# Later weights loaded from ScalarE's queue, weight products placed inside step 0, and a third buffer of turned rows

## The chip, the cores and the metric

The kernel runs on one core of one Trainium2 chip. That core has a TensorE for matrix products (PE in the rows), a VectorE (DVE), a ScalarE (ACT), a GpSimd (POOL) and a SyncE (SP) that only issues transfers, with 16 DMA engines behind them. The metric is the device time of one execution in microseconds. One profiled execution gives the trace that all rows are from; the times of three other runs are given beside it.

## The reference

The reference is one layer in three parts over `x`, 64 sequences of 64 tokens with 256 channels:

```python
x = x + _L0_xattn_ref(_layernorm(x, axis=-1), ctx_1024, mask, Wq, bq, Wk, bk, Wv, bv, Wo, bo)   # 16 heads, rotary, causal, 256 context rows
x = x + _L0_attn_ref(_layernorm(x, axis=-1), Wq, Wk, Wg1, Wg2, Wv, Wg, bg, Wo)                  # gated linear attention
x = x + _L0_ffn_ref(_layernorm(x, axis=-1), shared_gate, shared_up, shared_down,
                    routed_gate, routed_up, routed_down, Wr, routing_bias)                      # 1 shared + 7 routed experts, top 2
```

Two facts of it matter below. The keys' gate of the second part is `inputs @ Wg1 @ Wg2`, so a program can multiply the two weights once instead of twice per token. And the value bias `bv` of the first part passes through the softmax unchanged, so `bv @ Wo + bo` is one constant row that is added to the result. Each expert is `silu(x @ gate) * (x @ up) @ down` with 704 hidden channels, and each token's two routed results are added with its two weights.

## The kernel before

**Attention stage.** The 64 sequences go in 32 pairs, 128 tokens each. The work on one pair is cut into pieces (`turn_xn`, `proj_q`, `proj_k01`, `scores0`, ...), and each engine has a function `step(s)` that lists the pieces in a fixed order, each with a lag: `at(s, 2, weigh0)` runs `weigh0` on pair `s - 2`. There are 41 steps. Nothing but these lists and the semaphores sets the order; every engine takes its own list strictly in turn.

A pair starts like this: VectorE takes the statistics of its rows (`x_stats`, L1547), ScalarE makes the reciprocal deviation (L1121, L1123) and the high half of the context rows (`ctx_high`, L1224), GpSimd normalises (`x_norm`, L665) and makes the context's low half (`ctx_low`, L624). SyncE turns the split context rows by a transposing transfer (`turn_ctx`, L415). TensorE turns the normalised rows (`turn_xn`, L735), makes the queries (`proj_q`, L740), and then, with the turned context, the keys and values (`proj_k01`, `proj_k10`, `proj_v0`, `proj_k11`, all at L748). Matrix products are split in a high and a low half of 16 bits.

**Before the first step** each engine has a preamble. SyncE issues the loads in one queue: constants, the first context, `Wk`, `Wv`, their tables (`kv_loaded`), the first rows, the query weights, then 19 loads counted by `start_loaded` (L479: `Wg1`, `Wg2`, `bo` and `Wo` in 16 pieces) and 7 counted by `weights_loaded` (L484). ScalarE loads its table of functions (L1316), waits for `kv_loaded` and makes the high halves of `Wk` and `Wv` (L1319, L1320); VectorE makes the low halves and related copies (L1642 to L1654). TensorE waits for all 19 of `start_loaded`, turns `Wg1` (L1002), multiplies `bv` by `Wo` (L1005, recorded at L740) and `Wg1` by `Wg2` (L1008). VectorE copies and splits these results (L1657 to L1665), and only then comes to `x_stats` of pair 0, since it takes its list in turn.

**Expert stage.** 4096 tokens go through the shared expert in 16 tiles of 256, and 8192 choices (token, expert) through the routed experts in 35 tiles of 256, sorted by expert. The order of the 51 tiles is: tiles 0 to 9 shared, 10 to 44 routed (in each of the last four of these, each half has its own expert), 45 to 50 the last six shared. Each tile has on TensorE `up(t, half 0)`, `down(t - 1)`, `up(t, half 1)`: half 0 is 36 products of 128x256 at L1022, `down` 34 at L1050 to L1055, half 1 is 30 at L1022. In the trace half 1 of a tile and half 0 of the next stand in one row of 66.

The rows of a tile come to TensorE turned: `turn_rows(t)` on SyncE issues two transposing transfers (L531) into `e_rows_t[t % 2]`. It waits until tile `t - 2` has read this buffer (`up_done`, two counts per tile). For routed tiles GpSimd gathers the rows first (L694), and after the tile scatters the results to `choice_out` (L703). When tile 44 is done, GpSimd reads `choice_out` back in 8 transfers of 1 MB each (L721), and VectorE adds these results to the tokens (`combine`, L1907): one group of 8 operations beside tile 46, two beside each of 47, 48 and 49, one beside tile 50. The last transfers store the output (L725 on GpSimd, L562 on SyncE).

Of the kernel before, what the change touches and what calls it, by code (L numbers as in the profile page):

```python
# [6 lines left out]
ALU = mybir.AluOpType  # L7
# [4 lines left out]
F16 = mybir.dt.float16  # L12
# [33 lines left out]
LAST = 6  # L46
WORK = 9140
# [105 lines left out]
def program(nc, stack, x, ctx_in, pad, xWq, xbq, xWk, xWv, xWo, xbo, gWq, gWk, gWg1, gWg2, gWv,  # L153
# [134 lines left out]
    e_rows_t = [place2(2 * DK * R // 2).bitcast(F16).rearrange("p (m n) -> p m n", n=R) for _ in range(2)]  # L288
# [59 lines left out]
    for name in """  # L348
# [10 lines left out]
        route_exp route_mm route_step scores0_done scores1_done shared_hi shared_lo shared_loaded silu_ready  # L359
        slot_mm slots_loaded slots_read split_x2n_done start_loaded start_mm start_ready sum_decay_done  # L360
        sum_step table_ready turn_ctx_done turn_g_done turn_heads0_done turn_heads1_done turn_p00_done
        turn_p01_done turn_p10_done turn_p11_done turn_q_done turn_x1n_done turn_x2n_done turn_xn_done up_done
        v_hi0_done v_hi1_done v_lo0_done v_lo1_done waits_met weigh0_done weigh1_done weigh_g_done
        weights_loaded x1_norm_done x1_rstd_done x1_stats_done x1n_high_done x1n_low_done x2_norm_done
        x2_rstd_done x2_stats_done x2n_copy_done x_norm_done x_rstd_done x_stats_done xn_copy_done y_ready
        y_stored
# [5 lines left out]
    rows_turned = [sem(f"rows_turned{k}") for k in range(2)]  # L372
# [11 lines left out]
    def at(s, lag, op, first=0):  # L384
        if first <= s - lag < NPAIR:
            op(s - lag)
# [9 lines left out]
    def _(sp):  # L396
# [75 lines left out]
        first = [(w_g1, kmaj(gWg1)), (w_g2[0:16, :], gWg2), (b_o, xbo.partition_broadcast(P))]  # L472
        for hp in range(8):
            for a in range(2):
                row = (2 * hp + a) * HC
                first.append((w_o[hp * HC:(hp + 1) * HC, a, :], xWo[row:row + HC, :]))
        assert len(first) == START_DMAS
        for dst, src in first:
            sp.dma_start(dst, src).then_inc(S["start_loaded"], 16)  # L479
        wl = S["weights_loaded"]  # L480
        count = [0]

        def wload(dst, src):
            sp.dma_start(dst, src).then_inc(wl, 16)  # L484
            count[0] += 1

        wload(w_gqk[:, :, 0:P], kmaj(gWq))
        wload(w_gqk[:, :, P:2 * P], kmaj(gWk))
        wload(w_gvg[:, :, 0:D], kmaj(gWv))
        wload(w_gvg[:, :, D:2 * D], kmaj(gWg))  # L490
        wload(w_go, kmaj(gWo))
        wload(w_r, kmaj(Wr))
        wload(b_g[0:SQ, :], gbg.partition_broadcast(SQ))
        assert count[0] == WEIGHT_DMAS
# [50 lines left out]
        turn_tokens(1, 1)  # L545
        for t in range(FIRST):
# [4 lines left out]
            if t + 2 < FIRST:  # L551
                turn_tokens(t + 2, t + 2)
# [16 lines left out]
    def _(pool):  # L569
# [160 lines left out]
    def _(pe):  # L730
# [239 lines left out]

        def step(s):
# [12 lines left out]
            at(s, 0, turn_xn)  # L984
            at(s, 2, weigh1)
# [7 lines left out]
            at(s, 0, proj_k01)  # L993
            at(s, 0, proj_k10)
# [994 lines left out]
```

## Time and profile before

| | us |
|---|---|
| median of 3 runs | 1596.11 |
| lowest and highest of them | 1595.52, 1599.26 |
| profiled execution | 1593.83 |
| its span (first to last instruction) | 1592.0 |
| attention stage, expert stage, in the span | 0 to about 928, about 930 to 1592 |

The profiled execution is 1.83 us longer than its span; this lies around the span and isn't seen in the rows. It is 2.28 us below the median of the runs. Busy time is a sum over the whole span; a row of the timeline gives the start, the time and the idle time of the engine just ahead of it, with what ended that. A transfer's row on SPq (SyncE's queue) is only the time that it takes to issue it; when it lands is in other views.

### The profile page before, as it was taken

How to read it: one execution, taken by the hardware profiler on the slowest of the kernel's cores; microseconds unless marked ns; L12 is line 12 of the kernel's file. 1: busy time of each engine (PE TensorE's matmuls, PEld its weight loads, DVE VectorE, ACT ScalarE, POOL GpSimd, SP SyncE). 2: the span in 40 equal slices, each digit the busy share in tenths (PEclk: the TensorE clock that was granted, in tenths of full speed). 3: DMA queues.
4: the chain of work that ended last, by engine and by line, in shares of the span. 5: the costliest groups of instructions: out<-in, count | busy, mean ns of one | idle time of the engine just before them, and what ended most of it. 6: DMA issues, size and time to landing. Idle time of an engine off the chain costs nothing.

```text
span 1592.0 us, 43384 instructions
## 1 busy us (share of the span) xinstructions
PE 1434.0 (90%) x17186; PEld 1074.6 (68%) x17186; DVE 1085.5 (68%) x1972; ACT 847.2 (53%) x1838; POOL 761.4 (48%) x677
## 2 busy tenths in 40 slices
PE   3788998999999999999999665999999999999987
PEld 1456675666666666666666454887888888887865
DVE  2886889888888888888888459784444444443357
ACT  1566876777778777777687422452323232322221
POOL 1575677777677767676766310002333333332110
PEclk9899999999999999999999678999999999999998
DMA  4586776777677777767685343552422222221182
GB/s 136 115 167 125 148 136 124 141 132 144 137 139 142 137 149 135 150 129 146 119 155 97 74 101 70 139 156 70 74 67 74 68 74 68 74 68 55 38 267 74
DMA packets 464497, 183.62 MB, mean 115 GB/s; under 512 B 414608, under 2 KB 452832, under 8 KB 464304
## 3 DMA queue, kind: packets, MB, share of 16 engines
q1 hardware_dynamic: 454128, 149.25, 47.3%
q0 software_dynamic: 10176, 31.60, 5.7%
q8 instruction: 145, 2.38, 0.6%
q14 instruction: 48, 0.39, 0.1%
HBM read 61.77 MB, written 17.56 MB: 50 GB/s over the span
## 4 chain that ended last, share of the span: by engine, by line
PE 56%; DVE 24%; ACT 11%; issue 4%; DMA 3%; SPq 1%; POOL 1%; DVEq 0%; POOLq 0%
PE ps L1022 22%; PE ps L1050 10%; PE ps L748 9%; DVE experts L1392 6%; ACT experts L1128 4%; PE ps L740 4%; DVE work L1523 4%; ACT experts L1115 3%; PE ps L765 2%; DVE experts L1480 2%; PE ps L735 2%; PE ps L792 2%; DVE experts L1431 1%; DMA work<-token_in 1%; PE ps L1055 1%
## 5 line engine op out<-in xcount | busy, mean ns | idle before, releaser
L1022 PE MATMUL ps<-work,experts 128*128 128x256 f16 (+1 forms) x3630 | 403.7, 272 | 42.1 <-DMA work<-token_in 13.4
L1022 PEld LDWEIGHTS ps<-work,experts 128*128 (+1 forms) x3630 | 340.0, 100 | 97.6 <-issue 15.6
L748 PE MATMUL ps<-experts 128*128 128x512 f16 (+2 forms) x2304 | 363.8, 309 | 31.4 <-DVE work L1536 14.7
L748 PEld LDWEIGHTS ps<-experts 128*128 128x128 f16 x2304 | 198.2, 100 | 174.5 <-DVE work L1536 28.9
L1115 ACT ACTIVATE work<-work 128x768 f16<-128x768 f32 (+1 forms) x134 | 99.3, 741 | 368.5 <-PE ps L1055 234.4
L1128 ACT ACTIVATE experts<-ps,experts 128x256 f32<-128x256 f32 x512 | 203.8, 474 | 74.9 <-DVE experts L1392 74.8
L627 POOL TENSOR_TENSOR experts<-experts 128x1024 f16<-128x1024 f32 x96 | 191.7, 1996 | 61.0 <-ACT experts L1115 61.0
L694 POOL DMA_INDIRECT work<-token_in,work x70 | 68.0, 972 | 309.2 <-DMA work<-work 216.1
L1050 PE MATMUL ps<-experts,work 128*128 (+1 forms) x1530 | 187.8, 276 | 3.7 <-DVE work L1700 3.7
L1050 PEld LDWEIGHTS ps<-experts,work 128*128 128x128 f16 x1530 | 146.9, 99 | 28.7 <-DVE work L1700 4.0
L1392 DVE TENSOR_REDUCE experts<-ps 128x4 f32<-128x1024 f32 x128 | 155.9, 1219 | 12.7 <-PE ps L765 11.7
L1683 DVE SCALAR_TENSOR_TENSOR work<-ps,work 128x768 f32<-128x768 f32 x102 | 84.1, 824 | 115.9 <-PE ps L1022 115.4
L1115 ACT ACTIVATE experts<-experts 128x1024 f16<-128x1024 f32 x128 | 135.9, 1062 | 2.0
L703 POOL DMA_INDIRECT choice_out<-work x70 | 69.4, 992 | 134.9 <-DVE work L1841 123.7
L1696 DVE TENSOR_TENSOR work<-work 128x768 f16<-128x768 f32 x102 | 86.5, 848 | 58.7 <-ACT work L1115 58.7
L1334 ACT ACTIVATE work<-ps 128x768 f32<-128x768 f32 x102 | 82.5, 809 | 80.3 <-PE ps L1022 80.3
L748 PE MATMUL ps<-work,experts 128*128 128x33 f16 x3072 | 88.3, 178 | 23.1 <-issue 16.9
L748 PEld LDWEIGHTS ps<-work,experts 128*128 128x128 f16 x3072 | 86.0, 96 | 28.9 <-issue 28.1
L1841 DVE TENSOR_SCALAR work<-ps 128x512 f32<-128x512 f32 x35 | 24.2, 692 | 108.0 <-PE ps L1055 108.0
L740 PE MATMUL ps<-experts,work 128*128 128x256 f32 (+1 forms) x388 | 93.2, 360 | 2.7 <-ACT work L1115 1.7
L1431 DVE SCALAR_TENSOR_TENSOR experts<-ps,experts 128x512 f32<-128x512 f32 x128 | 88.8, 736 | 8.5 <-PE ps L748 8.5
L624 POOL TENSOR_TENSOR experts<-experts 128x1024 f16<-128x1024 f32 x32 | 72.2, 2256 | 16.6 <-ACT experts L1224 16.6
(211 smaller groups left out, 2184.4 us busy)
## 6 DMA issues: line engine op xcount, KB each, us to landing
experts<-in_ctx SPq DMA_DIRECT2D x32, 512.0 KB, 5.0
experts<-choice_out POOLq DMA_DIRECT2D x8, 1024.0 KB, 13.1
experts<-in_x SPq DMA_DIRECT2D x32, 128.0 KB, 2.3
token_in<-experts SPq DMA_DIRECT2D x32, 128.0 KB, 2.9
work<-in_L_ffn_routed_gate SPq DMA_DIRECT2D x8, 352.0 KB, 3.1
experts<-experts SPq DMA_TRANSPOSE x160, 4.6
work<-in_L_ffn_routed_up SPq DMA_DIRECT2D x8, 320.0 KB, 4.4
out<-x_all POOLq DMA_DIRECT2D x5, 512.0 KB, 3.3
```

The costliest lines, as they stand in the source:

```text
L627: nc.gpsimd.tensor_tensor(probs_s[b][m][:, 1, :], probs[b][:, 4 * m:4 * m + 4, :].rearrange("p s j -> p (s j)"), probs_s[b][m][:, 0, :], A ...
L740: ins = pe.matmul(bank, lhs[k], rhs[k], start=(k == 0), stop=(k == len(lhs) - 1))
L748: ins = pe.matmul(bank, lhs[a][k], rhs[b][k], start=(k == 0 and a + b == 0), stop=(last and k == len(lhs[0]) - 1 and a == 1))
L1022: ins = pe.matmul(out[:, r * n:(r + 1) * n], experts_h[:, e, lo:lo + P], e_rows_t[k][:, b * DK + kk, r * n:(r + 1) * n], start=(kk == 0 an ...
L1050: pe.matmul(out, e_hid_s[a][:, c, rows], experts_h[:, e, at:at + D], start=(c == 0 and a + b == 0), stop=False)
L1115: nc.scalar.activation(dst, src, ACT.Copy).then_inc(done, 1)
L1128: ins = nc.scalar.activation(probs[b][:, s, :], ps[:, r, g * SK:(g + 1) * SK], ACT.Exp, bias=neg_max[b][:, s:s + 1])
L1334: nc.scalar.activation(e_silu, ps_flat[:, 512 + half * HALF:512 + (half + 1) * HALF], ACT.Silu, scale=1 / W_SCALE).then_inc(S["silu_ready" ...
L1392: v.tensor_reduce(neg_max[b][:, 4 * m:4 * m + 4], ps_flat[:, 1024 * m:1024 * m + 1024].rearrange("p (s j) -> p s j", j=SK), AX.X, ALU.max, ...
L1431: v.scalar_tensor_tensor(out=dst.rearrange("p (b j) -> p b j", b=2), in0=bank.rearrange("p (b j) -> p b j", b=2), scalar=b_cols[:, 2 * e + ...
L1683: ins = v.scalar_tensor_tensor(out=e_hid[:, 0:n], in0=ps_flat[:, 2048 + half * HALF:2048 + half * HALF + n], scalar=1 / W_SCALE, in1=e_sil ...
L1696: ins = v.tensor_tensor(low, e_hid[:, 0:n], high, ALU.subtract)
```

## The change

There are three parts.

1. The 19 loads of `start_loaded` and the 7 of `weights_loaded` are issued by ScalarE, right behind its table load and ahead of its first ACTIVATE. SyncE goes from the query weights straight into its steps.
2. TensorE's three weight products leave the preamble. `start_turn` (the two transposes of `Wg1` and the product `bv @ Wo`) stands in step 0 behind `turn_xn`, `start_weight` (`Wg1 @ Wg2`) in step 0 behind `proj_k01`. VectorE's copies and splits become `start_bias` and `start_split` in step 1, behind `masks_of` and behind `q_cos` of pair 0. Some semaphores are merged for this (`shared_hi` into `kv_high`, `shared_lo` into `kv_split`).
3. `e_rows_t` has three buffers instead of two; `turn_rows(t)` waits for tile `t - 3`.

```diff
+NROWS = 3
@@ SyncE
-        first = [(w_g1, kmaj(gWg1)), (w_g2[0:16, :], gWg2), (b_o, xbo.partition_broadcast(P))]
...
-        for dst, src in first:
-            sp.dma_start(dst, src).then_inc(S["start_loaded"], 16)
...
         def turn_rows(t, rows):
-            wait(sp, S["up_done"], t * 2 - 2)
+            wait(sp, S["up_done"], 2 * (t - NROWS) + 2)
             apart(sp)
             for a in range(2):
-                sp.dma_start_transpose(e_rows_t[t % 2][:, :, a * P:(a + 1) * P], rows[a]).then_inc(rows_turned[t % 2], 16)
+                sp.dma_start_transpose(e_rows_t[t % NROWS][:, :, a * P:(a + 1) * P], rows[a]).then_inc(rows_turned[t % NROWS], 16)
-        turn_tokens(1, 1)
+        for t in range(1, NROWS):
+            turn_tokens(t, t)
...
-            if t + 2 < FIRST:
-                turn_tokens(t + 2, t + 2)
+            if t + NROWS < FIRST:
+                turn_tokens(t + NROWS, t + NROWS)
@@ GpSimd
         def residual(p):
-            if p == 0:
-                pool.wait_ge(S["start_ready"], 9)
         def gather(t):
             if t > FIRST:
-                pool.wait_ge(rows_turned[(t - 1) % 2], ((t - 1) // 2 + 1) * 32)
+                pool.wait_ge(rows_turned[(t - 1) % NROWS], ((t - 1) // NROWS + 1) * 32)
@@ TensorE
+        def start_turn(p):
+            pe.wait_ge(S["start_loaded"], 16 * START_DMAS)
+            pe.wait_ge(S["start_ready"], 7)
+            for k in range(DK):
+                pe.transpose(ps[0:16, 0, k * P:(k + 1) * P], w_g1[:, k, :], ident)
+            product(ps[:, 0, D:2 * D], [bv_rows[:, a, :] for a in range(2)], [w_o[:, a, :] for a in range(2)], S["start_mm"])
+
+        def start_weight(p):
+            pe.wait_ge(S["start_ready"], 8)
+            for k in range(DK):
+                ins = pe.matmul(ps[:, 2, k * P:(k + 1) * P], w_g1_t[0:16, k, :], w_g2[0:16, :], start=True, stop=True)
+            ins.then_inc(S["start_mm"], 1)
             at(s, 0, turn_xn)
+            at(s, 0, start_turn, 0, 1)
...
             at(s, 0, proj_k01)
+            at(s, 0, start_weight, 0, 1)
             at(s, 0, proj_k10)
         pe.wait_ge(S["consts_loaded"], 16)
-        pe.wait_ge(S["start_loaded"], 16 * START_DMAS)
...
@@ ScalarE
         act.preload_act_table_set("natural_log_exp_and_others")
+        for dst, src in first:
+            act.dma_start(dst, src).then_inc(S["start_loaded"], 16)
...
         act.wait_ge(S["consts_loaded"], 16)
         act.wait_ge(S["kv_loaded"], 64)
@@ VectorE
+        def start_bias(p):
+            dve.wait_ge(S["start_mm"], 1)
+            dve.wait_ge(S["start_loaded"], 16 * START_DMAS)
+            v.tensor_copy(w_g1_t[0:16], ps[0:16, 0, 0:DK * P].rearrange("p (k n) -> p k n", k=DK))
+            v.tensor_tensor(b_o, ps[:, 0, D:2 * D], b_o, ALU.add).then_inc(S["start_ready"], 1)
+
+        def start_split(p):
+            dve.wait_ge(S["start_mm"], 2)
...
             at(s, 1, masks_of)
+            at(s, 1, start_bias, 0, 1)
...
             at(s, 1, q_cos)
+            at(s, 1, start_split, 0, 1)
```

What the change moves is seen where each engine's instructions stand in a row. TensorE at its beginning, before:

```order
L1002 MATMUL ps<-cst,work 16x128 x2
L740 MATMUL ps<-experts,work 128x256 x2
L1008 MATMUL ps<-work 128x128 x2
L735 MATMUL ps<-cst,experts 128x128 x2
L740 MATMUL ps<-experts 128x256 x2
L748 MATMUL ps<-experts 128x512 x12
L748 MATMUL ps<-experts 128x256 x12
L748 MATMUL ps<-experts 128x512 x12
```

And of the change, the same place, where L951, the L716 on `experts,work` and L957 are the three weight products, L711 is `turn_xn` and the next L716 `proj_q`:

```order
L711 MATMUL ps<-cst,experts 128x128 x2
L951 MATMUL ps<-cst,work 16x128 x2
L716 MATMUL ps<-experts,work 128x256 x2
L716 MATMUL ps<-experts 128x256 x2
L724 MATMUL ps<-experts 128x512 x6
L957 MATMUL ps<-work 128x128 x2
L724 MATMUL ps<-experts 128x512 x6
L724 MATMUL ps<-experts 128x256 x12
L724 MATMUL ps<-experts 128x512 x12
```

The transposes and the `bv` product now stand between `turn_xn` and `proj_q`; `Wg1 @ Wg2` parts the first 6 products of `proj_k01` from the 6 of `proj_k10`.

VectorE from the end of its preamble, before (L1547 is the first statistics, L1486 `masks_of`, L1491 and L1495 the query's bias and cosine, L1431 the first rotated keys):

```order
L1653 COPY work<-experts 128x128 x2
L1654 TENSOR_SCALAR experts<-experts 128x4
L1657 COPY work<-ps 16x256
L1660 TENSOR_TENSOR experts<-ps,experts 128x256
L1663 TENSOR_SCALAR experts<-ps 128x256
L1665 SCALAR_TENSOR_TENSOR experts<-ps,experts 128x256
L1547 BN_STATS experts<-experts 128x6
L1550 BN_AGGR experts<-experts 128x2
L1486 SCALAR_TENSOR_TENSOR experts<-experts,cst 128x512
L1491 TENSOR_TENSOR experts<-ps,experts 128x256
L1495 TENSOR_TENSOR experts<-experts,cst 128x256
L1431 SCALAR_TENSOR_TENSOR experts<-ps,experts 128x512
```

And of the change (L1553 is the first statistics, L1608 and L1609 `start_bias`, L1614 and L1616 `start_split`):

```order
L1674 TENSOR_SCALAR experts<-experts 128x4
L1676 COPY work<-experts 128x128 x2
L1553 BN_STATS experts<-experts 128x6
L1556 BN_AGGR experts<-experts 128x2
L1492 SCALAR_TENSOR_TENSOR experts<-experts,cst 128x512
L1608 COPY work<-ps 16x256
L1609 TENSOR_TENSOR experts<-ps,experts 128x256
L1497 TENSOR_TENSOR experts<-ps,experts 128x256
L1501 TENSOR_TENSOR experts<-experts,cst 128x256
L1614 TENSOR_SCALAR experts<-ps 128x256
L1616 SCALAR_TENSOR_TENSOR experts<-ps,experts 128x256
L1437 SCALAR_TENSOR_TENSOR experts<-ps,experts 128x512
```

The four operations on the weight products went from ahead of the statistics to behind them, and the last two stand right ahead of the first rotated keys.

ScalarE behind its table load, of the change (before, the first ACTIVATE followed the table load at once):

```order
L1307 DMA work<-in_L_attn_Wg 128x2x16
L1307 DMA work<-in_L_attn_Wg 16x128
L1307 DMA experts<-in_L_xattn_bo 128x256
L1307 DMA experts<-in_L_xattn_Wo 16x256 x16
L1312 DMA experts<-in_L_attn_Wq 128x2x128
L1312 DMA experts<-in_L_attn_Wk 128x2x128
L1312 DMA experts<-in_L_attn_Wv 128x2x256
L1312 DMA experts<-in_L_attn_Wg 128x2x256
L1312 DMA experts<-in_L_attn_Wo 128x2x256
L1312 DMA experts<-in_L_ffn_Wr 128x2x7
L1312 DMA work<-in_L_attn_bg 64x256
L1325 ACTIVATE experts<-experts 128x2x256
```

All 26 loads stand ahead of the ACTIVATE that makes the high half of `Wk` (L1325), and so ahead of all that ScalarE does behind it. On SyncE nothing stands in another order but for the 26 loads that are gone and the two transposes of tile 2, which stand ahead of its loop; the transposes' waits are what changed.

## Rows read from the trace of the kernel before

**Rows 1.** The page: busy time by engine, and TensorE over 40 slices
```profile
PE 1434.0 (90%) x17186; PEld 1074.6 (68%) x17186; DVE 1085.5 (68%) x1972; ACT 847.2 (53%) x1838; POOL 761.4 (48%) x677
...
PE   3788998999999999999999665999999999999987
```

**Rows 2.** Waits of TensorE, 840:1592 (line, releaser: us, times, longest)
```profile
PE ps L1022 <- DMA work<-token_in: 13.4, 2, 7.4
```

**Rows 3.** Timeline, 0:60 (start, duration, engine, line, names, count, idle before)
```profile
0.73 1.28 ACT L1316 ACT_TABLE_LOAD   x1 [0.73 <-PEq L1975]
...
5.64 0.94 SPq L479 DMA_DIRECT2D work<-in_L_attn_Wg  x2
...
7.09 7.38 SPq L479 DMA_DIRECT2D experts<-in_L_xattn_Wo  x16
8.59 0.63 ACT L1319 ACTIVATE experts<-experts 128x512 f16<-128x512 f32 x1 [6.58 <-DMA experts<-constants]
...
11.66 0.17 DVE L1654 TENSOR_SCALAR experts<-experts 128x4 f32<-128x4 f32 x1
...
16.49 0.59 PE L1002 MATMUL ps<-cst,work 128*16 128x128 f32 x2 [16.49 <-DMA experts<-in_L_xattn_Wo]
...
17.54 0.57 SPq L484 DMA_DIRECT2D work<-in_L_attn_bg  x1
...
18.71 1.22 PE L1008 MATMUL ps<-work 16*128 16x128 f32 x4
...
20.77 0.42 DVE L1547 BATCH_NORM_STATS2 experts<-experts 128x6 f32<-128x256 f32 x1
...
24.81 2.07 PE L740 MATMUL ps<-experts 128*128 128x256 f32 x4 [0.47 <-ACT experts L1115]
...
30.07 8.64 PE L748 MATMUL ps<-experts 128*128 128x512 f16 x36 [3.19 <-DMA experts<-experts]
...
34.85 0.75 DVE L1431 SCALAR_TENSOR_TENSOR experts<-ps,experts 128x512 f32<-128x512 f32 x1 [7.04 <-PE ps L748]
```

**Rows 4.** 1100:1430: PE, PEld, DVE, ACT, POOL busy, PEclk, DMA, GB/s
```profile
1100.00:1430.00 330.00, 330.00 (x2913) 278.09 (x2912) 142.20 (x203) 94.76 (x116) 115.89 (x118) 1.00 0.28 71
```

**Rows 5.** Timeline, 1455:1592
```profile
1505.91 7.38 PE L1022 MATMUL ps<-work,experts 128*128 128x256 f16 x66
...
1510.93 5.72 POOL L721 DMA_DIRECT2D experts<-choice_out  x8 [1.71 <-DMA choice_out<-work]
...
1517.24 7.38 PE L1022 MATMUL ps<-work,experts 128*128 128x256 f16 x66
...
1528.58 3.45 PE L1022 MATMUL ps<-work,experts 128*128 128x256 f16 x30
...
1535.26 6.87 DVE L1907 SCALAR_TENSOR_TENSOR x_all<-experts,work,x_all 128x256 f32<-128x256 f32 x16
...
1539.46 5.71 PE L1022 MATMUL ps<-work,experts 128*128 128x256 f16 x36 [7.44 <-DMA work<-token_in]
...
1545.21 0.96 DVE L1683 SCALAR_TENSOR_TENSOR work<-ps,work 128x768 f32<-128x768 f32 x1 [3.08 <-PE ps L1022]
```

**Rows 6.** Timeline, 1552:1592
```profile
1562.71 0.96 DVE L1683 SCALAR_TENSOR_TENSOR work<-ps,work 128x768 f32<-128x768 f32 x1
...
1575.77 0.96 DVE L1683 SCALAR_TENSOR_TENSOR work<-ps,work 128x768 f32<-128x768 f32 x1
```

**Rows 7.** Chain that ended last, 900:1592 (start, duration, what)
```profile
1520.79 1.19 SPq L531
1522.02 17.40 DMA work<-token_in
```

**Rows 8.** DMA issues, 1508:1512 (count, KB each, median us to landing)
```profile
work<-token_in SPq DMA_TRANSPOSE x2, 4.4
```

**Rows 9.** Reads of choice_out, 1500:1592: issue durations (ns), and landing
```profile
L721 POOL DMA_DIRECT2D experts<-choice_out x8: 731/737/768, 1510.9 to 1515.9; - x8
...
DMA to landing us min/median/max: 2.4/11.1/22.1
```

More of the change, by code:

```diff
@@ L287, in program @@
     e_rows = place2(2 * D).rearrange("p (a d) -> p a d", a=2)
-    e_rows_t = [place2(2 * DK * R // 2).bitcast(F16).rearrange("p (m n) -> p m n", n=R) for _ in range(2)]
+    e_rows_t = [place2(2 * DK * R // 2).bitcast(F16).rearrange("p (m n) -> p m n", n=R) for _ in range(NROWS)]
     e_silu = place2(HALF)
@@ L371, in program @@
     x_loaded = [sem(f"x_loaded{k}") for k in range(3)]
-    rows_turned = [sem(f"rows_turned{k}") for k in range(2)]
+    rows_turned = [sem(f"rows_turned{k}") for k in range(NROWS)]
     chunk_loaded = [sem(f"chunk_loaded{k}") for k in range(5)]
@@ L382, in program, with at @@
     choices = choice_out[0:TOPK * NTILE * P, :].rearrange("(c p t) d -> p c t d", c=TOPK, p=P)
-    def at(s, lag, op, first=0):
-        if first <= s - lag < NPAIR:
+    def at(s, lag, op, first=0, last=NPAIR):
+        if first <= s - lag < last:
             op(s - lag)
@@ L999, in _ @@
         pe.wait_ge(S["consts_loaded"], 16)
-        pe.wait_ge(S["start_loaded"], 16 * START_DMAS)
-        for k in range(DK):
-            ins = pe.transpose(ps[0:16, 0, k * P:(k + 1) * P], w_g1[:, k, :], ident)
-        ins.then_inc(S["start_mm"], 1)
-        pe.wait_ge(S["start_ready"], 7)
-        product(ps[:, 2, 0:D], [bv_rows[:, a, :] for a in range(2)], [w_o[:, a, :] for a in range(2)], S["start_mm"])
-        pe.wait_ge(S["start_ready"], 8)
-        for k in range(DK):
-            ins = pe.matmul(ps[:, 1, k * P:(k + 1) * P], w_g1_t[0:16, k, :], w_g2[0:16, :], start=True, stop=True)
-        ins.then_inc(S["start_mm"], 1)
-        pe.wait_ge(S["start_ready"], 11)
         pe.wait_ge(S["fill_ready"], 1)
@@ L1027, in up @@
         def up(t, k, es, half):
-            wait(pe, rows_turned[t % 2], (t // 2 + 1) * 32)
+            wait(pe, rows_turned[t % NROWS], (t // NROWS + 1) * 32)
             blocks_of = range(half * HT // 2, (half + 1) * HT // 2)
@@ L1078, in _ @@
         for t in range(1, TABLE):
-            tile(t, t % 2, SHARED, SHARED)
+            tile(t, t % NROWS, SHARED, SHARED)
         pe.wait_ge(S["lane_hot_ready"], TOPK)
@@ L1093, in _ @@
         for t in range(TABLE, FIRST):
-            tile(t, t % 2, SHARED, SHARED)
+            tile(t, t % NROWS, SHARED, SHARED)
         pe.wait_ge(S["chunk_lo_ready"], NCHUNK * NE)
@@ L1316, in _, with kmaj, wload @@
         act.preload_act_table_set("natural_log_exp_and_others")
+        def kmaj(w):
+            return w.rearrange("(k p) n -> p k n", p=P)
+        first = [(w_g1, kmaj(gWg1)), (w_g2[0:16, :], gWg2), (b_o, xbo.partition_broadcast(P))]
+        for hp in range(8):
+            for a in range(2):
+                row = (2 * hp + a) * HC
+                first.append((w_o[hp * HC:(hp + 1) * HC, a, :], xWo[row:row + HC, :]))
+        assert len(first) == START_DMAS
+        for dst, src in first:
+            act.dma_start(dst, src).then_inc(S["start_loaded"], 16)
+        wl = S["weights_loaded"]
+        count = [0]
+        def wload(dst, src):
+            act.dma_start(dst, src).then_inc(wl, 16)
+            count[0] += 1
+        wload(w_gqk[:, :, 0:P], kmaj(gWq))
+        wload(w_gqk[:, :, P:2 * P], kmaj(gWk))
+        wload(w_gvg[:, :, 0:D], kmaj(gWv))
+        wload(w_gvg[:, :, D:2 * D], kmaj(gWg))
+        wload(w_go, kmaj(gWo))
+        wload(w_r, kmaj(Wr))
+        wload(b_g[0:SQ, :], gbg.partition_broadcast(SQ))
+        assert count[0] == WEIGHT_DMAS
         act.wait_ge(S["consts_loaded"], 16)
```

66 lines of the change are left out of this document (20 added, 46 removed).

## The prediction

> **What bounds the kernel now.** I read the page first: TensorE is busy in 1434.0 of 1592.0 us, and over the 40 slices it is at 9 tenths but for three places: the first two slices, the passage to the experts in the middle, and the last ones [rows 1]. The change touches the first and the last of these. In between the reader is to see that nothing is to be had: in 1100:1430, among the routed tiles, TensorE is busy in 330.00 of 330.00 us [rows 4], so an earlier transfer there ends no wait.
>
> Then I read TensorE's waits over the expert stage. It waited twice for turned tokens, 13.4 us in all, the longer 7.4 [rows 2]. The timeline shows where that is: ahead of half 0 of tile 48, started at 1539.46 after 7.44 us idle [rows 5]. The other 6.0 is tile 0's, at the very beginning of the stage. Its two transposes have no buffer to wait for and stand at the same place in the change, so it stays.
>
> Last the timeline of the beginning. TensorE's first instruction waits 16.49 us for `Wo`, whose 16 pieces SyncE issues in 7.38 us from 7.09 on; the VectorE is done with its preparations at 11.66 + 0.17 = 11.83, but comes to the first statistics only at 20.77, behind four operations that wait for the weight products [rows 3]. Those 8.9 us are what the start could give.
>
> **The loads on ScalarE.** SyncE took from 5.64 to 17.54 + 0.57 = 18.11, so 12.5 us, for these 26 issues, 0.48 each [rows 3]. ScalarE now pays them itself, and no row shows it issuing a transfer. Nearest rows: 0.48 for the same 26 on SyncE, 0.74 for one of GpSimd's plain reads [rows 9], 1.19 for a transpose on SyncE [rows 7]. I take 0.48, the same transfers. I put them behind the table load, which ends at 0.73 + 1.28 = 2.01 [rows 3]; if the issues go on beside it, it is 1.3 less. So ScalarE is free at 2.0 + 12.5 = 14.5. Before, it began with `Wk` at 8.59, when the tables had landed [rows 3]; the landing is 5.9 us ahead of 14.5, so even transfers that are slowed by the new neighbours are there in time. From ScalarE's first ACTIVATE to the end of VectorE's preparations it is 11.83 - 8.59 = 3.2 us. The first statistics then start at 14.5 + 3.2 = 17.7, against 20.77: 3.0 us earlier. The 8.9 are not had, since ScalarE's own queue has become what ends last.
>
> **The weight products in step 0.** From the statistics to the first product of `proj_k01` it is 30.07 - 20.77 = 9.3 us, by way of the statistics, normalising, `ctx_low` and the turned context, and TensorE waits 3.19 us for it behind `proj_q`, whose row ends at 24.81 + 2.07 = 26.88 [rows 3]. `start_turn` goes ahead of `proj_q`: from 16.49 to 18.71 it is 2.2 us with all waits in it [rows 3]. That fits into the 3.19, so it costs nothing; if the 3.19 were gone it would cost 2.2. Queued behind its wait on TensorE is only `proj_q`, and behind that the query's bias on VectorE, which has until 34.85: there VectorE has idled 7.04 us for the keys [rows 3]. The same idle time takes `start_bias`, and `start_split` runs beside `proj_k10`, so I cost VectorE's four operations at nothing. `start_weight` has no cover: it stands between `proj_k01` and `proj_k10`, the context is there by then, and the row of 36 products from 30.07 is busy without a gap [rows 3]. Its row is 1.22 us; I take -1.2. The bound on the other side is half of it, 0.6: the 36 products around it took 0.56 ns per column (8.64 us for 24 of 512 and 12 of 256), the 66 of a later row 0.44 (7.38 us for 256 each) [rows 3, 5], so its pace isn't fixed. 0 is excluded, since TensorE is in demand on both sides.
>
> The start gives 3.0 - 1.2 = 1.8 us. SyncE is 12.5 us of issuing lighter, but it waits for `ctx_low` next, and the next loads of context and rows come behind that as before. What shifts at the start shifts all steps behind, which wait only for each other.
>
> **The third buffer.** The transposes of tile 48 wait for tile 46's half 1 now. That is the first 30 products of the row of 66 that starts at 1517.24; SyncE issues the first at 1520.79, 1.19 us long, and what TensorE waits for lands 17.40 us after 1522.02 [rows 5, 7]. By then GpSimd has put 8 MB of reads into the queues, from 1510.93 on, which land up to 22.1 us after their issue [rows 5, 9]. That is the wait: a small transfer behind large ones. With three buffers the transposes of tile 48 wait for tile 45, the first 30 products of the row of 1505.91, so they are issued at about 1509.4, where those of tile 47 are now. The pair issued in 1508:1512 landed in 4.4 us (median) [rows 8], the second 1.2 behind the first: in place by 1516, against a need at 1528.58 + 3.45 = 1532.0 [rows 5]. The wait of 7.44 goes.
>
> What is late next? Tile 49's transposes take the place of tile 48's and land at 1539.5; TensorE wants them not ahead of 1544, since VectorE now comes first: beside tile 47 it combines two groups, 6.87 us from 1535.26, until 1542.13 [rows 5]. Only then can it take half 0 of tile 48, which it took at 1545.21 after 3.08 idle [rows 5]. So at tile 48 only 3.1 of the 7.4 is had. But before, half 0 of tile 49 was taken at 1562.71, 17.5 us after tile 48's, and that of tile 50 at 1575.77, 13.06 us after tile 49's, both with no idle time ahead [rows 6]. 13.06 is the pace of a VectorE that waits for nobody, with two groups per tile; the 17.5 holds 4.4 us in which it waited for `down` of tile 47, late behind the stall. At 13.06 per tile from 1542.13, tile 50 comes at 1568.25, 7.5 us ahead of 1575.77. Both ways of counting give the same; I take 7.4. The groups that it adds were issued by 1515.9 and landed by 1538.0 (1515.9 + 22.1) [rows 9], ahead of all uses that come earlier now.
>
> In the routed tiles the gathers may run one tile further ahead, beside a TensorE without a gap [rows 4]: nothing. In the first ten tiles the tokens' waits are tile 0's alone [rows 2]: nothing.
>
> **The sum** is 3.0 - 1.2 + 7.4 = 9.2 us. Against the profiled execution of 1593.83 this is 1584.6; its median stands 2.28 above that, so 1596.11 - 9.2 = 1586.9.
>
> **One generator for both queues (12%).** The rows at the start show one queue issuing at a time, without a gap, so they can't say whether two can issue side by side. If they can't, SyncE's own issues come between: 4.9 us for what it issues from the table load's start at 0.73 to 5.64, and 0.5 for the next rows [rows 3]. ScalarE's last ends at 0.7 + 4.9 + 0.5 + 12.5 = 18.6, the statistics come at 21.9, 1.1 later than before, and the sum is -1.1 - 1.2 + 7.4 = 5.1: 1591.0. For it: this queue's time per issue hardly depends on the size. Against it: nothing in the trace. The Trainium skill, "Perfetto Trace Analysis", section "DMA Instruction — HWDGE (DVE, Sync)", says that the block which writes the descriptors is shared by two sequencers and locked for exclusive use while it works; no row of this trace has two such queues at work, so it neither agrees nor disagrees.
>
> **VectorE takes the tail over (6%).** If after tile 48 the last tiles keep the spacing that they have, only the 3.1 us of idle time at 1545.21 are had [rows 5]: 3.0 - 1.2 + 3.1 = 4.9, 1591.2. For it: VectorE has no idle time ahead of tiles 49 and 50 [rows 6]. Against it: the 17.5 between 48 and 49, explained above.
>
> **The third buffer does nothing (4%).** The transposes would be earlier, but land no earlier, since the reads begin at 1510.93, 1.5 us behind their issue. Then 1.8 is left: 1594.3. Against it is the pair issued there, 4.4 us to landing [rows 8].
>
> **ScalarE issues dearly (14%), the slower side.** With a price of c per issue the statistics come at 2.0 + 26c + 3.2, and the whole change gives 20.8 - 5.2 - 26c - 1.2 + 7.4 = 21.8 - 26c. It decides at c = 0.84: above, the kernel is slower. At GpSimd's 0.74 [rows 9] it gives 2.6, so 1593.5, no change that can be told (8%). At 1.19, a transpose's price [rows 7], it is 9.1 slower: 1605.2 (6%, with all prices from about 1.0 on). For it: ScalarE has other work in its sequencer, and has never issued here. Against it: these are the same plain transfers as SyncE's 0.48.
>
> **The chances.** 64% for my forecast, which itself runs from 1583.1 (issues beside the table load, 1.3; `start_weight` at half, 0.6; the first 36 products at 0.44 ns per column if TensorE is busier ahead of them, 1.9) to 1589.0 (issues at 0.56, 2.1 more). A measurement of this kernel can tell about 0.3%, 4.8 us, from no change, so faster is below 1591.3. Faster: the 64, most of the one generator and of the tail (12 in all of their 18): 76%. Same: the rest of these, the buffer that does nothing, 0.74 per issue: 18%. Slower: 6%. The range for 8 in 10 is 1583 to 1592: it takes in one generator and the tail, and leaves out the dear issues and the useless buffer.
>
> **What would show it.** In the changed profile: 26 issues on ScalarE's queue at about 0.48 (or 0.74, or stretched while SyncE issues); the first ACTIVATE at 14.5 and the first statistics at 17.7; `start_turn` ended before the context lands, and 1.2 us between the keys' products; no wait of TensorE for `token_in` ahead of tile 48, and VectorE without idle time from tile 47's groups to the end; the last two tiles 13.06 us apart. Wrong would be: statistics behind 20.8, a wait for turned rows at tile 49 in place of 48, or a wait of VectorE for the read groups.

## The result, and the profile after

The changed kernel takes 1586.21 us (median of 7 runs, 1579.43 to 1590.85) against 1596.11 (7 runs, 1590.87 to 1603.16) on the same chip: ratio 0.9934, 95% interval 0.9909 to 0.9959 (the ratio compares all runs, so it is not quite that of the two medians). That is 9.9 us less, where 9.2 was forecast. The profiled execution took 1586.54 us, its span is 1584.7.

**The page.** TensorE's busy time falls by 6 us of 1434.0 at the same number of instructions; in the last slices one digit goes from 8 to 9 [rows 1].

```profile
PE 1427.9 (90%) x17186; PEld 1072.2 (68%) x17186; DVE 1083.9 (68%) x1972; ACT 848.2 (54%) x1838; POOL 763.1 (48%) x677
...
PE   3779998999999999999999766998999999999997
```

**The tail.** TensorE's waits from 840 to the end (line, releaser: total, times, longest). Of the two waits for turned tokens [rows 2] only tile 0's is left:

```profile
PE ps L1002 <- DMA work<-token_in: 6.1, 1, 6.1
```

The timeline of the stretch of [rows 5, 6] in the changed kernel (start, duration, engine and line, operation and names, count, idle time ahead):

```profile
1505.75 7.38 PE L1002 MATMUL ps<-work,experts 128*128 128x256 f16 x66
...
1510.78 5.74 POOL L697 DMA_DIRECT2D experts<-choice_out  x8 [1.71 <-DMA choice_out<-work]
...
1528.42 7.38 PE L1002 MATMUL ps<-work,experts 128*128 128x256 f16 x66
...
1535.10 6.87 DVE L1917 SCALAR_TENSOR_TENSOR x_all<-experts,work,x_all 128x256 f32<-128x256 f32 x16
...
1541.99 0.96 DVE L1693 SCALAR_TENSOR_TENSOR work<-ps,work 128x768 f32<-128x768 f32 x1
...
1543.01 1.48 PE L1002 MATMUL ps<-work,experts 128*128 128x256 f16 x12 [1.12 <-DVE work L1693]
...
1555.05 0.96 DVE L1693 SCALAR_TENSOR_TENSOR work<-ps,work 128x768 f32<-128x768 f32 x1
...
1568.11 0.96 DVE L1693 SCALAR_TENSOR_TENSOR work<-ps,work 128x768 f32<-128x768 f32 x1
```

The row of 1528.42 was cut at 30 products before, with 7.44 us of nothing behind; now it runs through its 66. VectorE takes half 0 of tile 48 without idle time, at the end of its two groups, and tiles 49 and 50 follow 13.06 us apart. TensorE now waits for VectorE, 1.12 us in tile 48: the engine that sets the pace has changed. From 1535.10 to tile 50's half 0 it is 33.01 us, before 1575.77 - 1535.26 = 40.51 [rows 5, 6]: 7.5 us less.

**The start.** The timeline of the beginning, where [rows 3] had 26 issues on SyncE:

```profile
0.74 1.28 ACT L1296 ACT_TABLE_LOAD   x1 [0.74 <-PEq L1985]
0.78 0.96 ACTq L1307 DMA_DIRECT2D work<-in_L_attn_Wg  x2
...
2.24 10.56 ACTq L1307 DMA_DIRECT2D experts<-in_L_xattn_Wo  x16
...
3.30 1.16 SPq L467 DMA_DIRECT2D experts<-constants  x1
...
4.98 1.64 SPq L405 DMA_DIRECT2D experts<-in_mask_BxS_bf  x1
...
15.92 0.53 ACTq L1312 DMA_DIRECT2D work<-in_L_attn_bg  x1
16.55 0.63 ACT L1325 ACTIVATE experts<-experts 128x512 f16<-128x512 f32 x1 [14.53 <-issue]
...
19.70 0.42 DVE L1553 BATCH_NORM_STATS2 experts<-experts 128x6 f32<-128x256 f32 x1
...
23.07 0.63 PE L951 MATMUL ps<-cst,work 128*16 128x128 f32 x2
...
23.50 1.91 PE L716 MATMUL ps<-experts,work 128*128 128x256 f32 x4
...
28.99 1.47 PE L724 MATMUL ps<-experts 128*128 128x512 f16 x6 [1.87 <-DMA experts<-experts]
...
30.39 0.71 PE L957 MATMUL ps<-work 16*128 16x128 f32 x4
...
31.03 5.37 PE L724 MATMUL ps<-experts 128*128 128x512 f16 x30
...
35.14 2.07 DVE L1437 SCALAR_TENSOR_TENSOR experts<-ps,experts 128x512 f32<-128x512 f32 x3 [0.86 <-PE ps L724]
```

ScalarE issues from 0.78 to 16.45, 15.7 us for the 26; the issues begin beside the table load. Its first ACTIVATE has waited for nothing but them (`issue`), and the statistics come at 19.70 against 20.77. `start_turn` (L951 and the first L716) ends ahead of the 1.87 us for the turned context, so it is hidden; `start_weight` (L957) stands in the row of keys at 0.71. The 36 products around it take 1.47 + 5.37 = 6.84 where they took 8.64 [rows 3].

**Where the start's gain went in this execution.** The last bias additions on the first keys start at 35.14. In the kernel before they stand here:

```profile
37.45 2.07 DVE L1431 SCALAR_TENSOR_TENSOR experts<-ps,experts 128x512 f32<-128x512 f32 x3 [0.86 <-PE ps L748]
```

So the changed kernel is 2.3 us ahead at the end of the first keys. But tile 0's first product in the expert stage starts at 935.18, against 934.03 before, 1.2 us behind, and the last row of 66 ahead of the tail, 1505.75, is only 0.16 ahead of 1505.91 [rows 5]. Busy times by stretch in the cross attention (stretch, its length, PE, PEld, DVE, ACT, POOL busy, granted clock of TensorE, DMA share, GB/s), first of the kernel before:

```profile
390.00:395.00 5.00, 5.00 (x142) 3.68 (x139) 4.56 (x13) 3.64 (x9) 4.38 (x5) 1.00 0.94 186
395.00:400.00 5.00, 3.88 (x71) 3.41 (x68) 3.12 (x6) 2.47 (x8) 4.58 (x4) 1.00 0.01 1
```

and of the changed one:

```profile
390.00:395.00 5.00, 3.45 (x68) 2.44 (x64) 3.42 (x8) 3.34 (x10) 4.34 (x3) 1.00 0.57 81
395.00:400.00 5.00, 5.00 (x48) 4.16 (x45) 2.21 (x5) 2.18 (x8) 1.89 (x2) 0.66 0.16 32
```

By the start of each pair's masking on VectorE the changed kernel led by 2.7 us at pair 14, ahead of these stretches, and trailed by 0.6 at pair 15, behind them: its TensorE was granted 0.66 of the full clock over 395:400 (2.4 GHz in part of it, 1.2 in the rest), where the kernel before had 1.00, and did 48 products while busy for all of the 5 us. By itself the fall costs (1 - 0.66) of 5 us, 1.7 of the 3.3 us by which the lead changed; what took the rest isn't shown. Such falls stand in every execution of this stage, some at the same place in all (the last 50 us of the stage have several), some in one alone. How much they shift shows in three kernels with the start as it was (the kernel before, buffer_only and reads_held): their statistics come within 0.4 us of each other, tile 0's first product at 934.03, 940.58 and 930.49, and the combining beside tile 47 begins at 1535.26, 1541.97 and 1531.52. So the 10 us between them arise in the attention stage. Its records of the lower clock from 30 us to tile 0 add up to 73.9, 80.7 and 67.2 us. Half of that is what they cost a TensorE that is always busy, so by this estimate they explain up to 6.7 of the 10.1 us. One profile can't price 2 us of the start. Stretches whose ends stand in both traces can be read from it, the rest from medians.

### The profile page after: what moved, and what is told of

Its sections match the earlier page's. It is cut to its first block, busy times and chain, and to the rows that moved or that the text cites. A ratio compares the mean times of both kernels' runs of the same rounds, so it can differ in the third digit from the quotient of the medians.

```text
span 1584.7 us, 43383 instructions
## 1 busy us (share of the span) xinstructions
PE 1427.9 (90%) x17186; PEld 1072.2 (68%) x17186; DVE 1083.9 (68%) x1972; ACT 848.2 (54%) x1838; POOL 763.1 (48%) x677
## 4 chain that ended last, share of the span: by engine, by line
PE 54%; DVE 25%; ACT 12%; issue 4%; DMA 2%; POOL 1%; ACTq 1%; another core or an unknown queue 0%; SPq 0%; DVEq 0%; POOLq 0%
PE ps L1002 21%; PE ps L1030 10%; PE ps L724 8%; DVE experts L1398 6%; ACT experts L1108 4%; DVE work L1529 4%; ACT experts L1095 3%; PE ps L716 3%; PE ps L741 2%; DVE experts L1486 2%; PE ps L768 2%; PE ps L711 2%; DMA experts<-experts 1%; DVE experts L1437 1%; PE ps L1035 1%
## 5 line engine op out<-in xcount | busy, mean ns | idle before, releaser
L724 PE MATMUL ps<-experts 128*128 128x512 f16 (+2 forms) x2304 | 360.3, 308 | 27.0 <-DVE work L1542 12.6
L1398 DVE TENSOR_REDUCE experts<-ps 128x4 f32<-128x1024 f32 x128 | 155.9, 1219 | 13.6 <-PE ps L741 12.5
L716 PE MATMUL ps<-experts,work 128*128 128x256 f32 (+1 forms) x388 | 92.6, 358 | 3.3 <-ACT work L1095 2.3
```

Of the source, the lines that this page charges most:

```text
L716: ins = pe.matmul(bank, lhs[k], rhs[k], start=(k == 0), stop=(k == len(lhs) - 1))
L724: ins = pe.matmul(bank, lhs[a][k], rhs[b][k], start=(k == 0 and a + b == 0), stop=(last and k == len(lhs[0]) - 1 and a == 1))
L1398: v.tensor_reduce(neg_max[b][:, 4 * m:4 * m + 4], ps_flat[:, 1024 * m:1024 * m + 1024].rearrange("p (s j) -> p s j", j=SK), AX.X, ALU.max, ...
```

## The experiments

Eight kernels, each named by its label. These are read from all profiles, in us: "statistics" is the first one's start, "keys" the start of the last bias additions on the first keys (35.14 above), "two groups" the start of the combining beside tile 47 (1535.10 above), and "tail" the time from there to tile 50's half 0.

```
                statistics   keys    two groups   tail    median   ratio to before, 95% interval
before            20.77     37.45     1535.26    40.51   1596.11
changed           19.70     35.14     1535.10    33.01   1586.21   0.9934 [0.9909, 0.9959]
buffer_only       20.70     37.28     1541.97    33.00   1590.12   0.9960 [0.9940, 0.9981]
start_only        19.79     38.50     1535.94    39.71   1591.20   0.9978 [0.9956, 1.0000]
products_only     11.54     31.51     1529.47    41.59   1586.99   0.9937 [0.9910, 0.9963]
sync_first        11.74     27.95     1521.65    32.99   1576.11   0.9878 [0.9853, 0.9904]
loads_only        23.42     39.63     1538.17    41.52   1595.62   0.9996 [0.9971, 1.0022]
alone             27.38     42.81     1537.93    33.01   1588.12   one run
reads_held        21.09     37.51     1531.52    32.99   1586.53   0.9937 [0.9917, 0.9958]
half_combine      19.14     34.56     1529.21    26.40   1574.17   one run
```

Each experiment's ratio is to runs of the kernel before that were made beside it, with medians of 1596.07 (24 runs) or, for the last four, 1596.42 (19 runs).

**buffer_only** and **start_only** split the change: the kernel before with the third buffer (two pairs of semaphores are merged for it, as in the change), and the changed kernel without it.

```
buffer_only, to the kernel before          start_only, to the changed kernel
+NROWS = 3                                 -NROWS = 3
-  for _ in range(2)]  (e_rows_t)          +NROWS = 2
+  for _ in range(NROWS)]
-  wait(sp, S["up_done"], t * 2 - 2)
+  wait(sp, S["up_done"], 2 * (t - NROWS) + 2)
```

> The kernel before with the third buffer alone (two pairs of semaphores merged to make room for its semaphore). If the end gives 7.4 us by itself: TensorE has no wait for token_in ahead of tile 48, VectorE takes half 0 of tile 50 13.06 us after that of 49, and the time is 7.4 us under before (ratio 0.995). If the tail is only worth VectorE's idle time, 3.1 us (0.998). If the start made the whole difference and the buffer nothing, 0 us. The first statistics stay at 20.8 us in all cases.

> The changed kernel with two buffers: loads on ScalarE and weight products in step 0 alone. If the start gives what the traces show at the end of the first keys (2.3 us), the time is 2 to 4 us under before (ratio 0.998), statistics at 19.7, and the wait of 7.4 us ahead of tile 48 is back. If the start is worth nothing by the end of the attention stage, as in the one trace of the changed kernel, the ratio is 1.000. If it holds the whole difference of the medians less the 7.4, the same 2.5 us.

The tail answers at once. TensorE's waits for turned tokens from 840 to the end in buffer_only:

```profile
PE ps L1024 <- DMA work<-token_in: 6.0, 1, 6.0
```

and in start_only:

```profile
PE ps L1002 <- DMA work<-token_in: 12.9, 2, 7.0
```

The wait and the 7.5 us of tail go with the third buffer alone, and come back without it. In medians buffer_only is 6.0 faster than before and start_only 4.9 (its interval just reaches no change), each against the runs beside it, together 10.8 against 9.9 measured for both. That each part is worth 5 us or so, rather than 7.4 and 1.8, lies within these intervals, some 3 us to each side.

**products_only** undoes the loads alone: two buffers, all 26 back on SyncE, and the weight products in step 0 as in the change.

```
-NROWS = 3
+NROWS = 2
-for dst, src in first:  act.dma_start(dst, src)...      (ScalarE)
+for dst, src in first:  sp.dma_start(dst, src)...       (SyncE, as before)
 at(s, 0, start_turn, 0, 1)
 at(s, 0, start_weight, 0, 1)
```

> Two buffers, weight products in step 0 and 1, but all 26 loads back on SyncE, as before. Theory A (ScalarE's own issuing is what ends last at the start): statistics at 11.9 us instead of 19.7, ScalarE's first ACTIVATE at 8.6, the turned context issued at 18.6 when SyncE has issued its loads, first product of the keys at about 23.2 instead of 29.0, and the time 6 to 7 us under before (ratio 0.996). Theory B (taking the loads off SyncE is what gives the start its gain): the first product of the keys is no earlier than 29.0, and the time is that of before or worse.

The statistics come at 11.54, 8.2 us ahead of the changed kernel's. But SyncE is busy with the loads until 18.24, so the context is turned late. The timeline of products_only:

```profile
11.54 0.42 DVE L1550 BATCH_NORM_STATS2 experts<-experts 128x6 f32<-128x256 f32 x1
...
17.67 0.57 SPq L484 DMA_DIRECT2D work<-in_L_attn_bg  x1
...
18.97 3.35 SPq L415 DMA_TRANSPOSE experts<-experts  x1
...
24.02 2.74 PE L747 MATMUL ps<-experts 128*128 128x512 f16 x6 [3.49 <-DMA experts<-experts]
```

Still its keys are 3.6 us ahead of the changed kernel's, and with two buffers its median, 9.1 under the kernel before (6 to 7 were expected, which is within its interval), is that of the whole change. So the earlier start comes from moving the products. The loads on ScalarE take part of it away: 8.2 us of the statistics, 3.6 of the keys.

**loads_only** makes the other half: the kernel before, with the 26 loads on ScalarE and the weight products where they were.

> The kernel before with the 26 loads issued by ScalarE alone: weight products in the preamble as before, two buffers. Theory A (ScalarE's own issuing now ends last): first ACTIVATE at 16.5 us, VectorE's preparations done at 19.8, then the products, statistics at 24.4 instead of 20.8, so about 3.6 us slower than before (ratio 1.002). Theory B (freeing SyncE helps): statistics at or ahead of 20.8, same or faster.

```
-for dst, src in first:  sp.dma_start(dst, src)...       (SyncE)
+for dst, src in first:  act.dma_start(dst, src)...      (ScalarE, behind the table load)
```

The timeline of loads_only:

```profile
15.62 0.58 PE L979 MATMUL ps<-cst,work 128*16 128x128 f32 x2 [15.62 <-DMA experts<-in_L_xattn_Wo]
16.14 0.63 ACT L1322 ACTIVATE experts<-experts 128x512 f16<-128x512 f32 x1 [14.12 <-issue]
...
19.36 2.07 PE L717 MATMUL ps<-experts,work 128*128 128x256 f32 x4 [3.15 <-DVE work L1656]
...
23.42 0.42 DVE L1550 BATCH_NORM_STATS2 experts<-experts 128x6 f32<-128x256 f32 x1
```

`Wo` lands 0.9 us earlier than at 16.49 [rows 3], which is all that the early issue brings here; TensorE then waits 3.15 for VectorE, whose preparations stand behind ScalarE's first work at 16.14. The statistics are 2.7 us later than before (3.6 were expected), the keys 2.2. The median can't tell it from no change.

**sync_first** is the version to which these two point: three buffers, the products in step 0, and on SyncE the 19 loads of the start ahead of the steps, the seven later weights behind the issues of step 2.

```
-for dst, src in first:  act.dma_start(dst, src)...      (ScalarE, with its 7 wload)
+for dst, src in first:
+    sp.dma_start(dst, src).then_inc(S["start_loaded"], 16)
 for s in range(STEPS):
     step(s)
+    if s == 2:
+        wload(w_gqk[:, :, 0:P], kmaj(gWq))
+        ...
```

> The changed kernel (three buffers, products in steps 0 and 1), but SyncE issues the 19 loads of start_loaded ahead of its steps and the 7 of weights_loaded behind step 2; ScalarE issues nothing. Theory A: statistics at 11.9, turned context issued at 16.6 and landed at 21.1, first product of the keys at 21.1, 8 us ahead of the changed kernel, and the time 15 to 18 us under before (ratio 0.990). If an early start is given back later (clock, or transfers that wait), no better than the changed kernel, 10 us under before (0.993).

Timeline of sync_first; the context is turned at 16.56, 8.0 us ahead of the changed kernel's 24.53:

```profile
11.74 0.42 DVE L1549 BATCH_NORM_STATS2 experts<-experts 128x6 f32<-128x256 f32 x1
...
16.56 1.89 SPq L415 DMA_TRANSPOSE experts<-experts  x1
...
21.06 2.21 PE L746 MATMUL ps<-experts 128*128 128x512 f16 x6 [0.17 <-DMA experts<-experts]
```

TensorE no longer waits for the context (0.17), and the keys are 7.2 us ahead of the changed kernel's. Its 1576.11 us (1571.81 to 1579.23, 6 runs) are 20.0 below the kernel before and 10.1 below the change, with intervals that don't touch: it beats both. That is more than the 15 to 18 expected. Its keys are 9.5 us earlier than before and its tail is 7.5 shorter, 17.0 together; the other 3 us lie within its interval (0.9853 to 0.9904, or 15 to 23 us).

**alone** asks why 26 issues took 15.7 us: ScalarE waits until SyncE has issued its own and they have landed.

```
+act.wait_ge(S["q_loaded"], 32)
 for dst, src in first:
     act.dma_start(dst, src).then_inc(S["start_loaded"], 16)
```

> The changed kernel, but ScalarE begins its 26 issues only when SyncE's own loads have landed, at about 12 us, so that one queue issues at a time. If the 15.8 us for 26 issues come from two queues that issue together, they take 12.5 here and none takes over 0.6; if they are ScalarE's own price for these transfers, they take 15 to 16 again, with single ones of 1.0 to 1.6. The start is late either way (first ACTIVATE at 24.5, or at 28).

Timeline of alone; `Wo`'s 16 issues take 7.51 us instead of 10.56, and all 26 take 24.13 - 11.52 = 12.6:

```profile
11.52 0.95 ACTq L1308 DMA_DIRECT2D work<-in_L_attn_Wg  x2
...
12.97 7.51 ACTq L1308 DMA_DIRECT2D experts<-in_L_xattn_Wo  x16
...
23.60 0.53 ACTq L1313 DMA_DIRECT2D work<-in_L_attn_bg  x1
```

So ScalarE's own price is 0.48 per issue, SyncE's of [rows 3]. The other 3.1 us come with SyncE's loads going on beside. The chain of waits shows ScalarE's long issues one by one (start, duration, what), in the changed kernel:

```profile
3.29 1.17 ACTq L1307
4.98 1.64 ACTq L1307
...
9.31 1.03 ACTq L1307
```

and in start_only, which begins alike:

```profile
7.99 1.58 ACTq L1307
```

The first two end with SyncE's 3.30 + 1.16 and 4.98 + 1.64 above. SyncE's issues of the same transfers in alone are 0.43 each. Most others of the two queues run side by side at their usual price, so neither queue waits for each issue of the other. The 1.03 has no issue of SyncE beside it, nor has the 1.58: SyncE's last one ended at 8.33 and at 7.47. So the two queues' issuing at one time isn't the whole cause. alone also waits until SyncE's loads have landed, so it doesn't part the issues from the transfers that are under way; which of them makes the long ones stays open.

alone's start is 7.7 us later than the changed kernel's, in the statistics as in the keys, and still its one run, 1588.12, lies within the changed kernel's 1579.43 to 1590.85. One run prices no start either.

**reads_held** tests what the wait at tile 48 was: the kernel before, two buffers, but GpSimd issues only three of its eight reads of 1 MB, and the other five when tile 48's turned rows have landed.

```
+if m == 3:
+    pool.wait_ge(rows_turned[(MID + 3) % 2], ((MID + 3) // 2 + 1) * 32)
```

> The kernel before, two buffers, but GpSimd issues the last 5 of the 8 reads of 1 MB only when the turned rows of tile 48 have landed. If the wait ahead of tile 48 is a small transfer behind large ones: these rows are issued at 1520.8 as before but land by 1526, TensorE's wait of 7.4 us is gone, the last two tiles are 13.1 us apart, and the time is 6 to 7.5 us under before (ratio 0.9955). If it is the two buffers and the late issue by itself, the wait stays at 5 to 7 us and the time is that of before.

Timeline of reads_held:

```profile
1507.19 2.23 POOL L723 DMA_DIRECT2D experts<-choice_out  x3 [1.71 <-DMA choice_out<-work]
...
1521.24 3.49 POOL L723 DMA_DIRECT2D experts<-choice_out  x5 [11.82 <-DMA work<-token_in]
...
1542.52 4.10 PE L1024 MATMUL ps<-work,experts 128*128 128x256 f16 x36 [1.60 <-DMA work<-token_in]
```

The same two transposes, issued at 1517.0 and 1518.3 into DMA engines that had by then all but finished the three reads (busy 0.33 in 1517:1519, 0.97 in 1514:1517), landed after 2.7 us each, against 17.4 with the eight reads ahead [rows 7]. Behind the five reads issued from 1521.24 on, tile 49's took 12.2 and 13.7 us and are late in their turn, by 1.60, but beside a VectorE that is behind anyway, so the tail is 32.99. The median, 9.9 below the runs beside it, is as good as that of the whole change: with intervals this wide it doesn't differ from buffer_only's.

**half_combine** tests who sets the pace of the tail.

```
-for t in range(m * GROUP, (m + 1) * GROUP):
+for t in range(m * GROUP, m * GROUP + 2):
```

> The changed kernel with half of VectorE's 64 additions of the routed results left out (two token tiles of each group of four). If VectorE sets the pace of the last tiles since the wait is gone, tiles 48 to 50 go at TensorE's 11.3 us instead of 13.06, half 0 of tile 50 is taken by VectorE at about 9 us less behind the start of the first group than the 44.1 us of the changed kernel, and the end comes 9 to 10 us sooner. If TensorE or a transfer sets it, the end moves by under 2.

Timeline of half_combine:

```profile
1529.21 3.70 DVE L1917 SCALAR_TENSOR_TENSOR x_all<-experts,work,x_all 128x256 f32<-128x256 f32 x8
...
1544.27 0.96 DVE L1693 SCALAR_TENSOR_TENSOR work<-ps,work 128x768 f32<-128x768 f32 x1
...
1555.61 0.96 DVE L1693 SCALAR_TENSOR_TENSOR work<-ps,work 128x768 f32<-128x768 f32 x1
```

The tiles are 11.33 us apart where they were 13.06, and the tail is 6.6 shorter: VectorE's additions set it, and 11.33 is where TensorE would. That is 3.2 us for the first pair of groups (6.87 to 3.70) and twice 13.06 - 11.33: from there on TensorE's pace stops the gain, which was expected to be about 9. This execution is 12.4 us shorter than the changed kernel's profiled one, but 5.9 of that stand ahead of the tail, where the two kernels are the same: that is the spread between executions.

## Why the prediction was right

**The time.** Forecast 1586.9, measured 1586.21. Part of that is luck. The tail's term was right. The start's 1.8 was 2.2 in the rows, but of three sizes that were all off: 1.07 for the statistics (forecast 3.0), 1.80 for the pace of the keys (forecast 0), -0.71 for `start_weight` (forecast -1.2).

**The third buffer, 7.4: right.** Measured 7.5 from the groups beside tile 47 to tile 50's half 0. All steps came as written: tile 48's rows landed in time, VectorE took half 0 at 1541.99 (forecast 1542.13), the pace was 13.06, tile 50 came at 1568.11 (1568.25). reads_held shows the cause as the prediction put it, a small transfer behind large ones, and half_combine the engine that is late next. One reading was a little off: of the 4.4 us between tiles 48 and 49 VectorE waited 3.14 for `down` of tile 47, the rest for half 1 of tile 48 behind it. The stall made both late, so the sum stands. The span's end shows 7.3 rather than 7.5 + 0.16: from tile 50's half 0 to the end it is 16.6 us in the changed profile and 16.2 before, and between 13.9 and 16.8 over all the kernels.

**ScalarE free at 14.5, statistics 3.0 us earlier: failed in size.** The step that failed is the sum 2.0 + 12.5: that the 26 issues cost ScalarE 0.48 each, as they had cost SyncE alone. They took 15.7 us beside SyncE's own loads, 3.1 more. That they start beside the table load, at 0.78 and not at 2.0, gave 1.2 back, and the end was 16.45. The statistics came 1.07 earlier, not 3.0. The rival of one generator pointed this way, but asked for 5.4 us (4.9 + 0.5), and for issues that take turns. The Trainium skill, "Perfetto Trace Analysis", section "DMA Instruction — HWDGE (DVE, Sync)", speaks of a block that is shared by two sequencers and locked for exclusive use while it works. This case agrees in part: long issues that end together (1.17 and 1.16, 1.64 and 1.64), but most ones side by side at 0.44 to 0.54 on either queue, and some long ones (1.03, and 1.58 in start_only) with none beside them.

**`start_turn` hidden: right.** The context was still awaited for 1.87 us behind `proj_q`.

**`start_weight`, 1.2: too much.** It took 0.71; the prediction had its other bound at 0.6.

**The pace of the first keys: put at nothing, worth 1.8.** The 36 products around `start_weight` took 6.84 and not 8.64, which stood only at the edge of the range ("if TensorE is busier ahead of them, 1.9"). That condition is what happened. Busy times of short stretches among these products (columns as in the result's section) show it. Of before:

```profile
32.00:34.00 2.00, 2.00 (x6) 0.72 (x5) 0.00 (x0) 0.00 (x0) 0.00 (x0) 1.00 0.03 6
34.00:36.00 2.00, 2.00 (x17) 1.45 (x16) 1.15 (x3) 0.00 (x0) 0.00 (x0) 1.00 0.00 0
```

of the changed kernel:

```profile
32.00:34.00 2.00, 2.00 (x17) 1.47 (x15) 1.44 (x4) 0.16 (x1) 0.00 (x0) 1.00 0.00 0
```

and of start_only, which has the changed kernel's start:

```profile
32.00:34.00 2.00, 2.00 (x6) 0.66 (x5) 0.80 (x2) 0.00 (x0) 0.00 (x0) 0.50 0.00 0
```

In start_only the granted clock is 0.50 there, 1.2 GHz, so 6 products take 2.00 us. The kernel before does the same 6 in its first row although the view prints 1.00. This 1.00 is not measured: the view prints it wherever the trace holds no record of the clock, and the first record, at 1.00 (2.4 GHz), begins only at 34.1 us before. From there on the row shows 17. In the changed kernel the first record begins at 27.2, ahead of the keys at 28.99, and their first six take 1.47 us. The first record and the pace go together in the other kernels too. In buffer_only (33.8), loads_only (35.8) and sync_first (22.6) it begins among the first keys, which are slow until then; in alone (35.3) it begins ahead of them, and they take 1.47 again. In products_only it begins at 20.0, but the clock falls to 0.50 from 23.4 to 26.9, and the first six keys, from 24.02 on, take 2.74.

What TensorE did ahead of that point differs as the prediction's condition says. In the changed kernel it worked from 22.62 to 27.11 without a pause of over 0.3 us, since `start_turn` fills the time between `turn_xn` and `proj_q`. Before, it paused 3.7 us ahead of `turn_xn`, 0.5 behind it and 3.2 ahead of the keys, and its clock rose only 4 us into them. So it is most likely `start_turn`, costed at nothing, that brings the 1.8 us. This is read from the rows of these kernels; no experiment moved `start_turn` by itself. Nor is it safe: in start_only the clock fell to 0.50 at 30.2, the 36 products took 1.67 + 7.91, and the keys came 1.1 us later than before.

**Dear issues on ScalarE (14%): wrong.** The price is 0.48 by alone, and 0.60 each (15.7 for 26) beside SyncE's loads, under the 0.74 where this rival began. **VectorE takes the tail over (6%)** and **the buffer does nothing (4%)**: wrong, by the tail's 7.5.

**What the prediction didn't ask.** It costed the loads and the products as one chain and never the change with one of them left out. loads_only and products_only show that they are of opposite sign: the statistics 2.7 us later with the loads alone, 9.2 earlier with the products alone. The 8.9 us "that the start could give" were there to have, with the loads left on SyncE: sync_first has the statistics 9.0 and the keys 9.5 us earlier than before. What stays open is how much of 9.9 us is the start's: the medians give 4.9 for start_only and 9.9 - 6.0 = 3.9 beside buffer_only, the profile 2.3 at the end of the first keys, and the intervals hold all of these.

## What to carry to other kernels

An engine that computes pays for each transfer that it issues, in line with its work; before loads are moved to "a free queue", ask what stands behind them there, and whether the loads were late at all. Here TensorE waited for `Wo` wherever it was issued from (16.49 before, 15.62 in loads_only, 16.89 in products_only), so moving the loads brought under 1 us, and what was late was the work that stood behind them ahead of the first step. Split a change into its parts on paper as on the chip: two of three parts can carry the third.

A small transfer that is issued behind megabytes of others lands behind them. Either issue it earlier, for which a buffer more is enough, or hold the large ones back.

Where executions of the same code differ by 10 us at a late landmark, read a gain over a stretch whose ends stand in both traces, and leave the sum to the medians.

## What the runs showed of the hardware

26 plain transfers issued by ScalarE took it 15.7 us while SyncE issued its own and these were under way, and 12.6 when they had landed. Most of the difference lies in a few issues of 0.9 to 1.6 us; some end on both queues together, some have none beside them. The table load and the issues of ScalarE run side by side (0.74 and 0.78). A transpose issued by SyncE took 3.35 us in products_only, where its seven weight loads had just been issued, and 1.89 to 2.10 in the other kernels.

Two small transposing transfers landed 2.7 us after their issue with little else under way, 12.2 and 13.7 behind 5 MB of reads, and the one that TensorE waited for 17.4 behind 8 MB, though the reads stand in another queue.

A granted clock of 1.00 in the view can mean that no record exists yet: up to the first record the products on the keys ran at the pace that they have at 0.50. The first record began between 20.0 and 35.8 us. The granted clock then fell to 0.50 at places that differ in part between executions of the same code.
